# GAT layer and normalised-adjacency layer on one core: x and adjacency also given transposed, row sums as products with ones, scores on VectorE

## The chip, the cores and the metric

The kernel runs on one core of a Trainium2 chip. The metric is the device time of one execution in microseconds, lower is better. Times come from runs on the chip, as a median. The host builds the input arrays before the launch, and its work is not in the time.

## The reference

Two layers on 2048 nodes with 512 features. `adj` is a 2048 x 2048 matrix of zeros and ones, with many more edges at low node numbers.

```python
def _L0_gnn_ref(x, adj, W_seq, a1, a2, W_out, b_out):      # N 2048, H 16, DH 32
    seq = (x @ W_seq).reshape(N, H, DH)
    score1 = jnp.einsum('nhd,d->hn', seq, a1)
    score2 = jnp.einsum('nhd,d->hn', seq, a2)
    scores = score1[:, :, None] + score2[:, None, :]
    scores = jax.nn.leaky_relu(scores, negative_slope=0.2)
    scores = scores + (1.0 - adj)[None, :, :] * -65500.0
    attn = jax.nn.softmax(scores, axis=-1)
    hidden = jnp.einsum('hij,jhd->ihd', attn, seq).reshape(N, D_IN)
    return jax.nn.elu(hidden @ W_out + b_out)
...
def adjacent_mat(adj):                                      # adj here: (A + A.T) * 0.5
    adj = adj + jnp.eye(adj.shape[0], dtype=adj.dtype)
    deg = jnp.sum(adj, axis=1)
    dinv = jnp.where(deg > 0, deg ** (-0.5), 0.0)
    return dinv[:, None] * adj * dinv[None, :]
...
x = _layernorm(x + L0(x, adj, ...))
x = _layernorm(x + adj @ (adjacent_mat((adj + adj.T) * 0.5) @ x))
```

A row of `adj` without edges gets a softmax over all nodes, since every score in it is lowered by the same amount.

## The kernel before

Nodes go in 16 tiles of 128 (NT = 16), features in 4 chunks of 128 (KC = 4). All engines run programs of their own, tied together by semaphores. There are four stages.

**Preparation.** For each tile t of 128 rows, SyncE loads 128 rows of `x` (0.25 MB) and 128 rows of `adj` (1 MB), each into two buffers in turn. TensorE transposes the x tile (`x_transpose`, line 469, 4 instructions), multiplies it by W_seq (`seq_product`, line 477, 4 products of 512 columns in float32, each of which the profile shows as two matmuls), multiplies it by WA (line 484, for the two scores; WA is W_seq contracted with a1 and a2, built by VectorE in lines 838 and 840), and transposes the mask tile 128 x 128 by 128 x 128 (`mask_tiles`, line 496, 16 instructions). ScalarE casts the adjacency tile to bfloat16 and takes its row sums (`cast_adj`, line 664), moves seq out of PSUM (line 668) and half of the transposed mask (line 672). VectorE moves the transposed x (line 848), marks edgeless rows from the row sums and fills them with ones in the mask (lines 853 to 858), adds the tile to a running column sum (line 862), moves the scores (line 864), takes the largest |seq| per head (line 869) and moves the other half of the transposed mask into `MT` as 8-bit codes (line 873). `MT[:, j, :]` holds the mask with the neighbour index j*128.. on partitions; a one is the byte 56, which is 1.0 in fp8.

**Between preparation and attention.** TensorE transposes the scores S1 (line 523), ScalarE moves them (line 687), SyncE stores them and loads them back broadcast to all partitions (`load_s1`). VectorE reduces the maxima (lines 890, 892), GpSimd takes the maximum over partitions with `partition_all_reduce` (line 414), VectorE and ScalarE build the tables of exponentials (lines 899 to 917, ending with `tabs_done`), GpSimd multiplies seq by the tables (`prep(0)`, line 421), ScalarE rounds the result (line 700), VectorE forms the low parts (`low_operands(0)`, lines 923 and 925, ending with `pn_ready`), then the degrees (lines 993 to 997, `deg_done`), and enters `att_head(0)`.

**Attention.** 16 heads of 16 steps. In a step j, a sign row is made by ScalarE (line 711, 10 of 16 steps, in 4 buffers) or by VectorE (`own_step`, line 959, issued one step ahead, 6 of 16 steps), VectorE ands it with `MT` (lines 970 and 974, `g_ready`) into one of 16 slots, and TensorE does 48 matmuls of 66 columns from that slot (lines 553 to 556, `g_used`). Within a head VectorE also evacuates the sums of the head before (lines 930 to 950) and builds operands for the next one (lines 923, 925), GpSimd prepares the one after that (line 421).

**Output and second layer.** Output projection, layer norm, and two products of 16 x 16 x 2 matmuls of 512 columns (line 628). `restore_and_add` takes the filled rows out of the mask again with the row `NEB`, which had gone through DRAM.

## Time and profile before

| | |
|---|---|
| median of 3 runs | 840.22 us (839.98 to 841.34) |
| the profiled execution | 840.77 us, of which the span is 839.0 us |
| TensorE matmul busy | 778.6 us (93%), 14113 instructions |
| VectorE busy | 641.7 us (76%) |
| ScalarE busy | 460.5 us (55%) |
| GpSimd busy | 104.4 us (12%) |
| HBM read, written | 61.37 MB, 8.65 MB |

How to read it: the span is the time from the first to the last instruction on the core, and the execution's own time is 1.8 us longer. Matmuls are pipelined, so a busy TensorE is not one at its peak; the distance from one matmul's start to the next says more than the duration of one. The profile cuts the span into 40 slices of 21 us and gives the busy share of each in tenths. In the chain of waits each piece is what the next one waited for.

### The profile page before, as it was taken

The page shows a single profiled execution, that of the slowest core. Times are in us where ns is not written, and L with a number is a line of the kernel's source. Part 1 is how long each engine was busy: PE and PEld are TensorE (multiplying, and loading weights), DVE is VectorE, ACT ScalarE, POOL GpSimd, SP SyncE. Part 2 cuts the span into 40 slices and gives each one's busy share as a digit, 9 for nine tenths or more (in the row PEclk, how much of TensorE's full clock was granted, in tenths as well). Part 3 has the DMA queues.
Part 4 walks back from the last instruction along what each step waited for, and adds up shares of the span by engine and source line. Part 5 has one row for each costly group of instructions (what it writes and reads, how often), then busy time and mean ns, then how long its engine had stood idle before and what let it go on. Part 6 is the DMA issues. An engine that isn't in the chain of part 4 may idle for free.

```text
span 839.0 us, 31365 instructions
## 1 busy us (share of the span) xinstructions
PE 778.6 (93%) x14113; PEld 581.9 (69%) x14113; DVE 641.7 (76%) x927; ACT 460.5 (55%) x376; POOL 104.4 (12%) x98
## 2 busy tenths in 40 slices
PE   1999956999999999999999998998799999999996
PEld 0666636999999999999999998443234444444442
DVE  5677859999999999999999973799956666344444
ACT  2565639988898888888988880466421111100000
POOL 1000013111111110111111200144300000000000
PEclk9999987999999999999999999899879999999999
DMA  6456535111111011111101111421515553011110
GB/s 239 175 210 242 187 104 224 54 54 54 55 54 34 24 55 54 54 55 54 53 18 43 54 66 41 115 63 50 137 51 150 150 150 100 6 43 40 39 38 38
DMA packets 46502, 71.85 MB, mean 86 GB/s; under 512 B 1952, under 2 KB 34720, under 8 KB 42144
## 3 DMA queue, kind: packets, MB, share of 16 engines
q1 hardware_dynamic: 46384, 70.03, 25.1%
q8 instruction: 104, 1.70, 0.9%
q14 instruction: 14, 0.11, 0.0%
HBM read 61.37 MB, written 8.65 MB: 83 GB/s over the span
## 4 chain that ended last, share of the span: by engine, by line
PE 55%; issue 36%; POOL 4%; DVE 3%; DMA 1%; ACT 0%; POOLq 0%; SPq 0%; DVEq 0%; ACTq 0%
PE bank L556 15%; PE bank L555 15%; PE bank L553 14%; PE bank L477 7%; POOL RZ L444 2%; PE bank L496 2%; PE bank L484 2%; POOL rstd L440 2%; PE bank L469 1%; DMA AV<-in_L_gnn_a_dram 1%; DVE RZ L959 1%; DVE W L838 1%; DVE WA L840 1%; DMA RZ<-in_x_dram 0%; POOL RP L421 0%
## 5 line engine op out<-in xcount | busy, mean ns | idle before, releaser
L553 PE MATMUL bank<-RP,RG 128*128 128x66 f16 x4096 | 387.1, 193 | 16.8 <-DVE RG L970 16.8
L553 PEld LDWEIGHTS bank<-RP,RG 128*128 128x128 fp8e4 x4096 | 386.1, 98 | 19.4 <-issue 19.4
L556 PE MATMUL bank<-RP,MT 128*128 128x66 f16 x4096 | 387.1, 194 | 2.3 <-issue 2.3
L555 PE MATMUL bank<-RP,RG 128*128 128x66 f16 x4096 | 387.1, 195 | 0.0
L556 PEld LDWEIGHTS bank<-RP,MT 128*128 128x128 fp8e4 x4096 | 386.1, 98 | 0.0
L555 PEld LDWEIGHTS bank<-RP,RG 128*128 128x128 fp8e4 x4096 | 386.0, 97 | 0.0
L711 ACT ACTIVATE RZ<-RZ,TAB 128x2048 int8<-128x2048 f32 x160 | 306.0, 1988 | 5.8 <-DVE RG L970 4.8
L959 DVE TENSOR_SCALAR RZ<-RZ,TAB 128x2048 int8<-128x2048 f32 x96 | 133.0, 1385 | 0.0
L628 PE MATMUL bank<-RG,RP 128*128 128x512 f16 x512 | 116.4, 388 | 8.8 <-DVE RG L1102 7.5
L970 DVE TENSOR_TENSOR RG<-RZ,MT 128x512 int32<-128x512 int32 x160 | 121.1, 757 | 0.0
L628 PE MATMUL bank<-RZ,MT 128*128 128x512 f16 x512 | 110.7, 379 | 0.0
L628 PEld LDWEIGHTS bank<-RG,RP 128*128 128x128 bf16 x512 | 49.8, 99 | 75.7 <-DVE RG L1102 11.2
L628 PEld LDWEIGHTS bank<-RZ,MT 128*128 128x128 fp8e4 x512 | 50.0, 98 | 60.5
L421 POOL TENSOR_TENSOR RP<-SEQ,TAB 128x528 f32<-128x528 f32 x32 | 53.0, 1676 | 286.5 <-DVE RP L925 279.5
L477 PE MATMUL bank<-RZ 128*128 128x512 f32 x128 | 61.4, 624 | 8.3 <-DVE RZ L848 8.3
L974 DVE TENSOR_TENSOR RG<-RZ,MT 128x512 int32<-128x512 int32 x96 | 65.2, 680 | 0.0
L820 ACT ACTIVATE W<-bank 128x512 f32<-128x512 f32 x16 | 9.6, 597 | 99.2 <-PE bank L628 99.2
L599 PE MATMUL bank<-RZ 128*128 128x512 f32 x128 | 59.7, 611 | 0.0
L440 POOL TENSOR_TENSOR rstd<-vps,mhalf 128x1 f32<-128x1 f32 x32 | 21.1, 660 | 285.3 <-DVE vps L1093 217.5
L801 ACT ACTIVATE W<-bank,DSL 128x512 f32<-128x512 f32 x16 | 11.0, 687 | 75.0 <-PE bank L628 75.0
L1183 DVE SCALAR_TENSOR_TENSOR W<-bank,W 128x512 f32<-128x512 f32 x16 | 11.1, 691 | 51.7 <-ACT W L820 51.7
L700 ACT ACTIVATE RP<-RP 128x1056 f16<-128x1056 f32 x16 | 18.0, 1126 | 55.8 <-PE bank L556 49.3
(112 smaller groups left out, 672.0 us busy)
## 6 DMA issues: line engine op xcount, KB each, us to landing
RG<-in_adj_dram SPq DMA_DIRECT2D x16, 1024.0 KB, 4.9
RZ<-s_rows_dram SPq DMA_DIRECT2D x16, 1024.0 KB, 4.9
RP<-in_adj_dram SPq DMA_DIRECT2D x16, 1024.0 KB, 5.9
RZ<-in_x_dram SPq DMA_DIRECT2D x32, 256.0 KB, 2.6
seq_copy_dram<-SEQ SPq DMA_DIRECT2D x1, 4224.0 KB, 18.3
out_dram<-W SPq DMA_DIRECT2D x16, 256.0 KB, 2.0
RZ<-in_L_gnn_W_seq_dram SPq DMA_DIRECT2D x1, 1024.0 KB, 5.3
RZ<-in_L_gnn_W_out_dram SPq DMA_DIRECT2D x1, 1024.0 KB, 5.5
```

What stands on the lines that cost most here:

```text
L421: gp.tensor_tensor(V2[:, :, e, :], SEQ[:, :, h, :], tab[:, h, :].unsqueeze(2).broadcast_to([P, NT, DV]), ALU.mult).then_inc(v2_ready, 1)
L440: gp.tensor_tensor(rstd[:, u:u + 1], vps[:, u:u + 1], mhalf[:, 0:1], ALU.pow).then_inc(done, 1)
L477: last = mm(pb[2 + u][:, :], xT[:, u, k * P:(k + 1) * P], WS[:, k, :], start=(k == 0), stop=(k == KC - 1))
L553: mm(pb[bank][:, c:c + 2 * DV], step, high, start=(j == 0 and i % IB == 0), stop=(j == NT - 1), skip_group_check=True)
L555: mm(pb[bank][:, c:c + 2 * DV], step, low, start=False, stop=(j == NT - 1), skip_group_check=True)
L556: last = mm(pb[bank][:, c + DV:c + 3 * DV], mask, edge, start=False, stop=(j == NT - 1), skip_group_check=True)
L599: last = mm(pb[2 + u][:, :], hT[:, u, k * P:(k + 1) * P], WO[:, k, :], start=(k == 0), stop=(k == KC - 1))
L628: last = mm(pb[4 + 2 * u + l][:, :], stationary(j), moving[:, l, j, :], start=(j == 0), stop=(j == NT - 1))
L711: A(Z[:, m % NZ, :], S1B[:, u, :], ACT.Sign, bias=S2[:, h, j:j + 1], scale=-1.0).then_inc(z_ready, 1)
L959: V.tensor_scalar(ZD[:, (h * len(OWN) + m) % 2, :], S1B[:, u, :], S2[:, h, OWN[m]:OWN[m] + 1], -1.0, ALU.is_gt, ALU.mult).then_inc(zd_read ...
L970: V.tensor_tensor(G32[:, s, :], Z32[:, m % NZ, :], MT32[:, j, :], ALU.bitwise_and).then_inc(g_ready, 1)
L974: V.tensor_tensor(G32[:, s, :], ZD32[:, m % 2, :], MT32[:, j, :], ALU.bitwise_and).then_inc(g_ready, 1)
```

## The change

The host passes `x` and `adj` a second time, transposed (`x_t`, `adj_t`). The kernel reads `x_t` in 4 groups of 4 tiles (1 MB each) into four buffers, W_seq in 4 chunks, and 16 tiles of `adj_t` (1 MB each) into four buffers. ScalarE casts each tile of `adj_t` straight into `MT` as fp8, which also gives the column sums `CS`. Row sums come from 64 products of ones with `MT` (512 columns each), accumulated in 4 PSUM banks. The scores are products and a reduction on VectorE from seq. The maxima over partitions go through a TensorE transpose, a VectorE reduction, and a product with the identity that broadcasts them. Edgeless rows are found from the row sums (`find_empty`, `EMP`) and ored into `MT` in `fill_empty`, one step ahead within head 0; `restore_and_add` xors them away. The degrees move behind head 0, the scale factors ahead of head 15, and the flag for the rare general path is computed on VectorE alone. The x transposes, the mask transposes, the WA product, both `partition_all_reduce` and the trip of `NEB` through DRAM are gone.

```diff
@@ sync @@
-            for u in range(2):
-                load_x(u, u)
-                load_adj(u, u)
-            with sp.Fori(1, NT // 2) as p:
...
+            def load_adj(t):
+                if t >= NA:
+                    sp.wait_ge(adjb_done, t - NA + 1)
+                sp.dma_start(adj_f[:, t % NA, :], adj_t[t * P:(t + 1) * P, :]).then_inc(adj_in[t % NA], 16)
+            load_x(0)
+            for k in range(KC):
+                sp.dma_start(WS[:, k, :], w_seq[k * P:(k + 1) * P, :]).then_inc(wseq_in[k], 16)
...
+            load_adj(0)
+            load_x(1)
+            for t in range(1, NA):
+                load_adj(t)
+            load_x(2)
+            for t in range(NA, 2 * NA):
+                load_adj(t)
+            load_x(3)
+            for t in range(2 * NA, NT):
+                load_adj(t)
@@ gpsimd @@
-            gp.partition_all_reduce(VC[:, :], red[:, :, :].rearrange("p e h -> p (e h)"), P, RMAX).then_inc(allred, 1)
...
@@ tensor @@
+            for n in range(NT):
+                seq_product(n)
+                if n >= 2:
+                    score_row(n - 2)
+            row_sums(0, 4)
+            score_row(NT - 2)
+            score_row(NT - 1)
+            row_sums(4, 6)
+            pe.wait_ge(red_done, 1)
+            pe.wait_ge(seq_sb, NT)
+            tr(pb[0][0:3 * H, 0:P], red[:, :], idf[:, :]).then_inc(red_ps, 1)
+            row_sums(6, 8)
+            pe.wait_ge(top_sb, 1)
+            mm(pb[1][:, 0:3 * H], TOPB[:, :], idf[0:3 * H, 0:3 * H], start=True, stop=True).then_inc(top_ps, 1)
+            row_sums(8, 12)
...
+            for t in range(NT):
+                last = tr(pb[7][:, t:t + 1], ROWR[0:1, t * P:(t + 1) * P], idf[0:1, 0:1])
@@ scalar @@
+            def cast_adj(t):
+                sc.wait_ge(adj_in[t % NA], (t // NA) * 16 + 16)
+                A(MT8[:, t, :], adj_f[:, t % NA, :], ACT.Copy, saturate=False, accum_out=CS[:, t:t + 1]).then_inc(adjb_done, 1)
...
+            for n in range(NT):
+                move_seq(n)
+                if n % GT == 2 and n > GT:
+                    move_s1(n // GT - 1)
+                cast_adj(n)
+            move_s1(NT // GT - 1)
...
             high_operands(0)
+            for k in range(KC):
+                sc.wait_ge(emp_sb, k + 1)
+                A(ROWR[0:1, k * 512:(k + 1) * 512], pb[4 + k][0:1, :], ACT.Copy).then_inc(rowr_sb, 1)
@@ vector @@
+            def scores(t):
+                seq_t = SEQ[:, t, :, 0:DH]
+                ve.wait_ge(seq_sb, t + 1)
+                V.tensor_reduce(VMT[:, t, :], seq_t, AX.X, ALU.max, apply_absolute_value=True).then_inc(vm_done, 1)
+                if t >= 1:
+                    ve.wait_ge(s_sb, t)
+                V.tensor_tensor(PRD, seq_t.unsqueeze(1).broadcast_to([P, 2, H, DH]),
+                                AV[:, :, :].unsqueeze(2).broadcast_to([P, 2, H, DH]), ALU.mult).then_inc(products_done, 1)
+                ve.wait_ge(products_done, t + 1)
+                V.tensor_reduce(TAB[:, 0:2, :, t], PRD, AX.X, ALU.add).then_inc(s_sb, 1)
...
+                    if h == 0:
+                        if j < NT - 1:
+                            fill_empty(j + 1)
+                        ve.wait_ge(mt_full, j + 1)
                     ve.wait_ge(g_used, h * NT + (j + 1))
...
+            def find_empty(k):
+                ve.wait_ge(row_ps, k + 1)
+                V.tensor_scalar(EMP[:, k * 512:(k + 1) * 512], pb[4 + k][:, :], 0.0, ONE8, ALU.is_equal, ALU.mult).then_inc(emp_sb, 1)
+            def fill_empty(j):
+                V.tensor_tensor(MT32[:, j, :], MT32[:, j, :], EMP32, ALU.bitwise_or).then_inc(mt_full, 1)
             low_operands(0)
+            for k in range(KC):
+                find_empty(k)
+            ve.wait_ge(emp_sb, KC)
+            fill_empty(0)
+            att_head(0)
```

## Rows read from the trace of the kernel before

**Rows 1.** The profile's page: TensorE's busy tenths in 40 slices; DMA issues (KB, us to landing).

```profile
PE   1999956999999999999999998998799999999996
...
RG<-in_adj_dram SPq DMA_DIRECT2D x16, 1024.0 KB, 4.9
RP<-in_adj_dram SPq DMA_DIRECT2D x16, 1024.0 KB, 5.9
RZ<-in_L_gnn_W_seq_dram SPq DMA_DIRECT2D x1, 1024.0 KB, 5.3
```

**Rows 2.** Chain that ended last (start us, length us, what): one tile, last tile.

```profile
26.96 3.59 PE bank L477 x8
30.55 0.81 PE bank L484 x8
31.37 0.47 PE bank L469 x4
31.84 0.89 PE bank L496 x16
...
111.71 0.81 PE bank L484 x8
```

**Rows 3.** Groups by line and form, 0 to 125 us (busy us, mean ns).

```profile
L664 ACT ACTIVATE RZ<-RG 128x2048 bf16<-128x2048 f32 x16 | 30.4, 1903 | 10.9 <-DMA RG<-in_adj_dram 10.9
...
L848 DVE COPY RZ<-bank 128x512 f32<-128x512 f32 x16 | 11.1, 691 | 2.8 <-PE bank L469 2.8
...
L838 DVE TENSOR_TENSOR W<-RZ,AV 128x2048 f32<-128x2048 f32 x2 | 4.6, 2292 | 8.7 <-DMA AV<-in_L_gnn_a_dram 8.6
...
L869 DVE TENSOR_REDUCE RP<-SEQ 128x16 f32<-128x512 f32 x4 | 2.7, 674 | 0.0
```

**Rows 4.** Timeline 112 to 133 us: between preparation and attention.

```profile
115.09 0.41 DVE L892 TENSOR_REDUCE red<-TAB 128x16 f32<-128x256 f32 x1
...
117.32 0.29 DVE L905 TENSOR_SCALAR TAB<-TAB 128x256 f32<-128x256 f32 x1
...
119.75 0.07 DVE L917 MEMSET RD<- 128x16 f32 x1
...
123.07 2.12 POOL L421 TENSOR_TENSOR RP<-SEQ,TAB 128x528 f32<-128x528 f32 x2 [6.99 <-issue]
...
127.83 0.44 DVE L925 TENSOR_SCALAR RP<-RP 128x1056 f16<-128x1056 f16 x1
...
128.38 1.06 DVE L995 TENSOR_SCALAR ROW<-ROW 128x16 f32<-128x16 f32 x1
...
132.43 0.21 PE L553 MATMUL bank<-RP,RG 128*128 128x66 f16 x1 [16.78 <-DVE RG L970]
```

**Rows 5.** VectorE's timeline in attention: heads 0 to 2, head 15.

```profile
130.39 1.27 DVE L959 TENSOR_SCALAR RZ<-RZ,TAB 128x2048 int8<-128x2048 f32 x1
131.59 0.70 DVE L970 TENSOR_TENSOR RG<-RZ,MT 128x512 int32<-128x512 int32 x1
132.21 0.68 DVE L974 TENSOR_TENSOR RG<-RZ,MT 128x512 int32<-128x512 int32 x1
...
150.56 1.27 DVE L959 TENSOR_SCALAR RZ<-RZ,TAB 128x2048 int8<-128x2048 f32 x1
...
207.09 0.71 DVE L930 TENSOR_TENSOR RP<-bank,TAB 128x528 f32<-128x528 f32 x1 [0.83 <-PE bank L556]
...
498.05 0.71 DVE L930 TENSOR_TENSOR RP<-bank,TAB 128x528 f32<-128x528 f32 x1 [5.00 <-PE bank L556]
```

**Rows 6.** Window 136 to 137 us (us, busy by engine, PEclk, DMA share, GB/s).

```profile
136.00:137.00 1.00, 1.00 (x35) 1.00 (x33) 1.00 (x1) 1.00 (x1) 0.00 (x0) 0.96 1.11 473
```

**Rows 7.** Window 9 to 10 us (columns as in Rows 6).

```profile
9.00:10.00 1.00, 0.55 (x3) 0.58 (x4) 1.00 (x1) 0.00 (x0) 0.00 (x0) 1.00 1.04 442
```

**Rows 8.** Timeline (start us, us, engine line op): first tile's product.

```profile
18.83 5.96 PE L477 MATMUL bank<-RZ 128*128 128x512 f32 x8 [8.29 <-DVE RZ L848]
```

**Rows 9.** GpSimd, line 421, 110 to 200 us: what stood ahead of it.

```profile
L421 POOLq MODIFY_POOL_CONFIG  x2: 99/99/99, 116.0 to 116.1; - x2
```

More of the change, by code:

```diff
@@ L462, in _ @@
             mm, tr = nc.tensor.matmul, nc.tensor.transpose
[L463 to L474 removed]
+            pe.wait_ge(consts, 5)
@@ L529, in _, with score_row @@
-            pe.wait_ge(tiles_added, NT)
-            for j in range(NT):
-                last = mm(pb[7][:, j:j + 1], CSA[:, j * P:(j + 1) * P], ones[:, 0:1], start=True, stop=True)
-            last.then_inc(col_ps, 1)
+            def score_row(t):
+                g = t // GT
+                pe.wait_ge(s_sb, t + 1)
+                if g >= 2 and t % GT == 0:
+                    pe.wait_ge(s1T_sb, g - 1)
+                last = tr(pb[2 + g % 2][0:H, (t % GT) * P:(t % GT + 1) * P], S1[:, :, t], idf[:, :])
+                if t % GT == GT - 1:
+                    last.then_inc(s1T_ps, 1)
@@ new lines, in row_sum, with row_sums @@
+            def row_sum(t, k):
+                last = mm(pb[4 + k][:, :], ones[:, :], MT8[:, t, k * 512:(k + 1) * 512], start=(t == 0), stop=(t == NT - 1))
+                if t == NT - 1:
+                    last.then_inc(row_ps, 1)
+            def row_sums(lo, hi):
+                for t in range(lo, hi):
+                    pe.wait_ge(adjb_done, t + 1)
+                    for k in range(KC):
+                        row_sum(t, k)
+            for n in range(NT):
+                seq_product(n)
+                if n >= 2:
+                    score_row(n - 2)
@@ L909, in _ @@
+            own.mark(V.tensor_copy(SEQ[:, :, :, DH], VM.unsqueeze(1).broadcast_to([P, NT, H])))
+            own.mark(V.reciprocal(RV[:, :], VM))
             own.wait(ve)
@@ L1018, in _ @@
             ve.wait_ge(dscale, 3)
-            for h in range(2, H):
-                att_head(h)
+            att_head(H - 1)
             scale_sums(H - 1)
```

302 lines of the change are left out of this document (85 added, 217 removed).

## The prediction

> **What bounds the kernel now.** I read the page's 40 slices first: TensorE stands at 9 or above from slice 3 to 23, which is preparation and attention [rows 1]. Busy matmuls say little, so the chain that ended last comes next. It runs through preparation on TensorE alone, tile after tile: 3.59 us for the seq product, 0.81 for WA, 0.47 for the x transposes, 0.89 for the mask transposes, 5.76 us in all, and the last seq product ends at 111.71 us, where the last WA product starts [rows 2]. I call this moment T. The other engines have room: ScalarE's cast is 1.90 us of each tile, and of VectorE's operations the move of the transposed x is 0.69 and the largest |seq| 0.67 [rows 3].
>
> From T to the first attention matmul at 132.43 there are 20.7 us, a chain of small steps over all engines: maxima ready at 115.50 (115.09 + 0.41), tables' input at 117.61, `tabs_done` at 119.82, GpSimd's first product only at 123.07, `pn_ready` at 128.27, first matmul 132.43 [rows 4].
>
> In attention VectorE's timeline shows who leads. It waits for TensorE at line 930, the first evacuation of the head before: at 207.09 for head 2, at 498.05 for head 14. So a head takes TensorE (498.05 - 207.09) / 12 = 24.25 us. VectorE did its own head 0 from 130.39 to 150.56, 20.2 us, and is ahead of TensorE [rows 5]. Attention costs 24.25 us a head whatever VectorE does, as long as it keeps this lead. At the start TensorE ran at half its clock (1.2 of 2.4 GHz) from 132.43 until 136, for 3.6 us, so half of that, 1.8 us, was lost [rows 4, 6]. After attention nothing of the change lies on the path: a xor takes the place of an and of the same form.
>
> **Part 1, the preparation.** Removed from TensorE: WA, x and mask transposes, 2.17 us of 5.76 a tile. Added in the loop: one score transpose a tile; the four x transposes take 0.47 us, so one is 0.12 us [rows 2]. What is left is the seq product: between 3.4 us (an estimate: 3.59 less some 0.2 for the turn to another kind of product) and the 3.59 of the chain. I take 3.5, since nothing but one short transpose stands between two products.
>
> Who could be late instead? ScalarE: cast 1.90 + the seq move, under 0.7 = 2.6 us [rows 3]. VectorE: largest |seq| 0.67; the two score operations work on 1024 elements, and the one in line 838 takes 2.29 us for 2048, so at most 1.25 each with the start of an operation in it: 3.2 us a tile [rows 3]. This is under 3.6, but only by 0.4 us. Between the two ends (half of 2.29, all parallel: 2.9; a full 1.6 each for the odd strides: 3.9) I take 3.2. DMA: 1 MB of W, 4 of x, 16 of adjacency are 22.0 MB. With several loads queued 442 GB/s is moved, at a busy share of the DMA engines of 1.0 [rows 7]. Then 22.0 MB take 50 us, inside 58. The last buffers are asked for four tiles ahead, 14 us, while one load lands in 4.9 us when little else is queued [rows 1]. SyncE's queue holds the x loads behind adjacency loads that wait for casts; the latest, for tile 12, is behind load 7, which waits for cast 3, long before tile 12. So DMA is hidden.
>
> The Trainium skill speaks against this ("DMA: Bandwidth & Descriptors", "Where 436 GB/s comes from": the HBM side binds at some 358 GB/s for each core). By it the 22.0 MB would need 61 us, the last moves of seq would stand behind casts that wait for loads, and the sum would be about 1 us longer. The measured 442 GB/s decides.
>
> Start: W (1 MB) lands 5.3 us after its issue at about 0.7, at 6.0 [rows 1]. Now x group 0, of the same size and run length, is issued there, and the first quarter of W follows 0.6 us later (0.26 MB at 442 GB/s): 6.6. The clock is low at first: the first product took 5.96 against 3.59, so 2.4 us more [rows 2, 8]. T = 6.6 + 2.4 + 16 x 3.5 + 14 x 0.12 = 66.7 us (65.1 with 3.4; 68.2 with 3.59). Before it was 111.7: 45.0 us less.
>
> **Part 2, from T to attention.** The old steps and the new, each with the same kinds of rows:
> - To maxima ready: 3.8 us before. Now the seq move 0.65, the three score operations 3.1, and four small reductions and a negation instead of two reductions, 1.8: 5.5.
> - To the tables' input: 2.1 before, with GpSimd's all-reduce in it. Now two trips through PSUM: transpose 0.3, reduction 0.3, copy 0.2; then TensorE stands behind `row_sums(6, 8)`, 8 matmuls of 0.21 us (512 columns at 2.4 GHz) = 1.7, which is longer than VectorE needs; product 0.3, then five small operations 1.4: 3.8.
> - Tables: 2.2, unchanged [rows 4].
> - GpSimd's answer to `tabs_done`: before 3.25 us (119.82 to 123.07) although it stood idle [rows 4]. Ahead of the product stand two MODIFY_POOL_CONFIG at 116.0 [rows 9], just behind the all-reduce; 116.0 to 123.1 is a change of code. Without the all-reduce there is none: 0.1.
> - GpSimd, ScalarE, VectorE to `pn_ready`: 5.2 (123.07 to 128.27), unchanged [rows 4].
> - `pn_ready` to first matmul: 4.2 before [rows 4]. Now four `find_empty` of 512 elements from PSUM, each 0.6 (0.69 from line 848, about 0.08 less from start to start, like the ands at 131.59 and 132.21, 0.62 apart), then `fill_empty` 0.6, own_step 1.2, `fill_empty` 0.6, and 0.7, waits 0.2: 5.8 [rows 3, 5]. ScalarE's copies and first sign row (four copies in step with `find_empty`, then 0.6 and 2.0) end at 5.1, just in time.
>
> The sum is 22.6 us against 20.7. In the old path the little operation of line 995 took 1.06 us, about 0.9 too long, while GpSimd was at work on `prep(1)`, and another like it followed [rows 4]. If `find_empty` is held up in the same way it costs 1.7: 22.6 to 24.3. I take 23.0, near the low end, as `find_empty` reads PSUM and the one of line 995 reads SBUF. By the Trainium skill ("SBUF — State Buffer", "Who interferes with whom") an operation of VectorE with at most one SBUF input outside the two-port modes isn't held up by GpSimd, so that the sum would be 22.6; no row shows the case. The row sums are hidden: 64 x 0.21 = 13.7 us on TensorE from T, while `find_empty` asks for them at T + 16.8. The stored scores, two transfers that have 17 us, too.
>
> First attention matmul: 66.7 + 23.0 = 89.7, against 132.43: 42.7 us earlier.
>
> **Part 3, head 0.** VectorE gets 15 more `fill_empty` of 0.6 = 9.0 us. Its 20.2 us held about 1.7 of GpSimd's interference, which now falls behind head 0 with `deg_done`: 27.5 us. TensorE needs 24.25 + 1.8 for the low clock = 26.1. Step by step, VectorE first falls behind at step 12, after the low operands (1.6 us): slot 12 is ready 20.7 us after slot 0, and TensorE gets to it at 19.9; the slot for step 13 comes 2.4 us later against 1.5. Together 1.65 us are lost by the end of the head (0 if the fills run at 0.5; 4 if GpSimd's interference stays in head 0 and doubles). In head 1 VectorE works 22.7 us against 24.25 and is ahead again. `deg_done` now comes about 20 us later; behind it on GpSimd are the power (4.2) and `prep(2)`, for whose result ScalarE may wait 2 us in head 1; its four sign rows in store cover that. The scale factors, moved ahead of head 15, fall where VectorE waits 5.0 us for TensorE [rows 5].
>
> **Sum.** 42.7 - 1.65 = 41.0 us. The profiled execution took 840.77 (span 839.0, 1.8 around it), 0.55 above the median of the runs: 840.77 - 41.0 = 799.8, and against the median 799.2.
>
> **The rivals.**
> - VectorE bounds preparation (its tile 3.9 instead of 3.2): 16 x 0.3 = 5 us more, 804. For: only 0.4 us of room. Against: all pieces are continuous streams of shapes seen.
> - DMA paces preparation at 300 GB/s instead of 442: 73 us of load, 4.5 of start, last cast at 81, and ScalarE holds the seq moves behind the casts; T is then at about 78: 811. For: the 22 MB now come in 58 us, far denser than before. Against: rows 7.
> - GpSimd still answers 3.2 us late: 802.5.
> - TensorE starves in head 0 and its clock stays at the low level through it: 48 matmuls of 66 columns at 1.2 GHz are 2.64 us a step, 42.2 us a head, so 18 more: 817.
> - Slower than before: the loads don't overlap, and each MB takes what the strided adjacency loads take alone, 5.9 us [rows 1]. 21 x 5.9 + 4.5 = 128 us to the last load; the last seq move waits for the cast before the last, at 125; attention starts 22 us later, at 147, which is 14.6 us later than now, and head 0 adds 1.65: 857. It decides from 5.1 us for each MB, about 205 GB/s.
>
> **Chances.** Forecast 0.70, VectorE 0.10, DMA 0.08, GpSimd 0.05, clock 0.04, slower 0.03. The forecast's bounds: T 65.1 to 68.2, part 2 22.6 to 24.3, head 0 0 to 4: 795.5 to 804. With the rivals next to it the range is 794 to 811. Faster 0.96, within 0.2% 0.01, slower 0.03; 0.2% is about what a measurement here can tell from no change.
>
> **What would show it.** Distances of 3.5 to 3.6 us between seq products and the last one ended at 67; VectorE's tile of 3.2 us; GpSimd's product within 0.2 us of `tabs_done`; 23 us from T to the first matmul, 26 to 30 us for head 0 and 24.25 for each one after. If seq products wait for the seq move, or the moves for casts behind loads, part 1 is wrong; if VectorE waits never return in heads 1 to 3, part 3 is.

## The result, and the profile after

The changed kernel takes 798.5 us, the median of 4 runs (797.52 to 800.07), against 840.1 for the kernel before, measured beside it (839.85 to 841.34). The ratio is 0.9504, 95% interval 0.9485 to 0.9522. The prediction said 799.2, range 794 to 811. The profiled execution has a span of 797.1 us, 41.9 less than the 839.0 of before. I split these 41.9 at the first and the last product of attention.

First the page of the changed kernel: busy tenths of TensorE and the DMA engines in 40 slices of 20 us, then the loads of the adjacency (KB each, median us from issue to landing).

```profile
PE   6999799999999999999999997989699999999996
...
DMA  7992510111111011111011214122345551011111
...
RG<-in_adj_t_dram SPq DMA_DIRECT2D x16, 1024.0 KB, 10.6
```

Against rows 1, TensorE's gap has moved from slice 6 to slice 5, and a load of the adjacency takes 10.6 us to land instead of 4.9 or 5.9. The loads now lie close together, and the DMA digits of slices 2 and 3 are 9.

The chain that ended last (start us, length us, what), from the first product to the last scores.

```profile
7.03 12.96 PE bank L451 x24
20.09 3.44 PE bank L451 x8
23.53 0.11 PE bank L460
23.64 3.44 PE bank L451 x8
...
62.63 3.45 PE bank L451 x8
...
68.59 1.23 DVE TAB L796
```

This answers rows 2: where a tile was 5.76 us of four kinds of work, it is now one seq product and one score transpose (line 460), 3.545 us in the mean of 12 tiles ((62.63 - 20.09) / 12), and TensorE alone is on the chain for all 16 tiles. T, the end of the last seq product, is 62.63 + 3.45 = 66.1 us, against 111.7.

These 45.6 us have two parts. TensorE's first product starts at 7.03 instead of 18.83 us (rows 8), and from there to T it is 59.05 instead of 92.88. So 33.8 us come from the tiles and 11.8 from the start. In the kernel before, the chain of the start was the load of the attention vectors, then four operations of 2.3 us on VectorE that build WA, then the move of the first transposed x, which stood behind them in VectorE's program (the load and the first of the four):

```profile
1.78 6.74 DMA AV<-in_L_gnn_a_dram
...
8.62 2.30 DVE W L838
```

With WA gone, TensorE waits for x and the first quarter of W alone.

The timeline of the stretch behind it (start us, us, engine, line, operation; in brackets the idle time before it, and what ended it) answers rows 4.

```profile
70.98 0.42 DVE L809 TENSOR_REDUCE red<-TAB 128x16 f32<-128x256 f32 x1
...
74.10 0.21 DVE L817 COPY VC<-bank 128x48 f32<-128x48 f32 x1 [1.54 <-PE bank L488]
...
75.22 0.29 DVE L824 TENSOR_SCALAR TAB<-TAB 128x256 f32<-128x256 f32 x1
...
77.65 0.07 DVE L836 MEMSET RD<- 128x16 f32 x1
77.80 2.13 POOL L404 TENSOR_TENSOR RP<-SEQ,TAB 128x528 f32<-128x528 f32 x2 [75.51 <-DVE RD L836]
...
82.83 2.48 DVE L914 TENSOR_SCALAR EMP<-bank 128x512 int8<-128x512 f32 x4
82.99 2.10 POOL L404 TENSOR_TENSOR RP<-SEQ,TAB 128x528 f32<-128x528 f32 x2 [3.06 <-DVE RP L844]
...
88.79 0.22 PE L515 MATMUL bank<-RP,RG 128*128 128x66 f16 x1 [0.95 <-DVE RG L893]
```

The first attention matmul is at 88.79 instead of 132.43: 43.6 us earlier, 45.6 at T less 2.0 between T and attention (22.7 instead of 20.7). From there to VectorE's last evacuation it is 392.5 us (481.31 - 88.79) instead of 389.7 (522.12 - 132.43): 2.8 given back. What follows is 1.1 us shorter. 43.6 - 2.8 + 1.1 = 41.9.

Where the 2.8 are is read from the start of every 768th attention matmul, which begins a head (us for a head):

| head | 0 | 1 | 2 | 3 | 4 | 5 to 13 | 14 | 15 |
|---|---|---|---|---|---|---|---|---|
| before | 26.27 | 24.10 | 24.08 | 24.07 | 24.08 | 24.07 to 24.08 | 26.12 | 24.09 |
| changed | 27.68 | 25.01 | 24.34 | 24.07 | 24.80 | 24.07 to 24.08 | 25.67 | 24.09 |

Head 0 has 1.4 more and head 1 has 0.9 more. The differences of heads 4 and 14 (0.7 more, 0.5 less) are in stops in which TensorE waits for no semaphore; experiment 7 is about them. The 0.3 of head 2 is in no single wait. In heads 0 and 1 two things are seen. TensorE's granted clock is at its lower level, 1.2 GHz, for 5.0 us (to 93.8) instead of 3.6 (windows: us, busy us by engine, granted clock, DMA share, GB/s):

```profile
93.00:94.00 1.00, 1.00 (x25) 1.00 (x23) 1.00 (x3) 1.00 (x2) 0.00 (x0) 0.59 0.00 0
94.00:95.00 1.00, 1.00 (x38) 1.00 (x35) 1.00 (x3) 1.00 (x1) 0.00 (x0) 1.00 0.00 0
```

And TensorE waits for VectorE three times behind its first matmul, 1.3 us in all (the wait of 0.95 at 88.79 is ahead of it and so already counted):

```profile
109.57 0.20 PE L515 MATMUL bank<-RP,RG 128*128 128x66 f16 x1 [0.36 <-DVE RG L897]
...
111.97 0.20 PE L515 MATMUL bank<-RP,RG 128*128 128x66 f16 x1 [0.71 <-DVE RG L893]
...
136.96 0.20 PE L515 MATMUL bank<-RP,RG 128*128 128x66 f16 x1 [0.18 <-DVE RG L893]
```

The last of them is in head 1. Which of the two, clock or VectorE, sets the length of these heads is told by experiment 7: VectorE.

### The profile page after: what moved, and what is told of

Its sections match the earlier page's. It is cut to its first block, busy times and chain, and to the rows that moved or that the text cites. A ratio compares the mean times of both kernels' runs of the same rounds, so it can differ in the third digit from the quotient of the medians.

```text
span 797.1 us, 30149 instructions
## 1 busy us (share of the span) xinstructions
PE 756.9 (95%) x13731; PEld 552.4 (69%) x13731; DVE 617.8 (78%) x864; ACT 446.8 (56%) x364; POOL 96.4 (12%) x94
## 3 DMA queue, kind: packets, MB, share of 16 engines
q1 hardware_dynamic: 46064, 69.77, 25.4%
## 4 chain that ended last, share of the span: by engine, by line
PE 48%; issue 38%; DVE 7%; POOL 4%; DMA 1%; ACT 0%; POOLq 0%; SPq 0%; DVEq 0%; ACTq 0%
PE bank L518 14%; PE bank L517 13%; PE bank L515 13%; PE bank L451 7%; DVE RZ L878 2%; POOL RZ L423 2%; POOL rstd L419 2%; DVE RG L893 1%; DVE MT L918 1%; DVE RG L897 1%; DMA RZ<-in_L_gnn_W_seq_dram 1%; DMA RZ<-in_x_dram 0%; DVE RP L842 0%; PE bank L465 0%; DVE EMP L914 0%
## 5 line engine op out<-in xcount | busy, mean ns | idle before, releaser
L561 PE MATMUL bank<-RZ 128*128 128x512 f32 x128 | 59.2, 607 | 0.2 <-ACT RZ L678 0.2
L451 PE MATMUL bank<-RZ 128*128 128x512 f32 x96 | 44.9, 621 | 7.0 <-DMA RZ<-in_L_gnn_W_seq_dram 7.0
L561 PEld LDWEIGHTS bank<-RZ 128*128 128x128 f32 x128 | 23.7, 196 | 25.1 <-issue 23.8
## 6 DMA issues: line engine op xcount, KB each, us to landing
RG<-in_adj_t_dram SPq DMA_DIRECT2D x16, 1024.0 KB, 10.6
RZ<-in_x_t_dram SPq DMA_DIRECT2D x3, 1024.0 KB, 11.8
```

Of the source, the lines that this page charges most:

```text
L451: last = mm(pb[t % 2][:, :], XT[t // GT][:, k, (t % GT) * P:(t % GT + 1) * P], WS[:, k, :], start=(k == 0), stop=(k == KC - 1))
L561: last = mm(pb[2 + u][:, :], hT[:, u, k * P:(k + 1) * P], WO[:, k, :], start=(k == 0), stop=(k == KC - 1))
```

## The experiments

The kernel before, measured anew beside each set, took 839.1 to 841.4 us, so that times of different sets can be compared to some 0.3%, 2.3 us; where less matters, the traces decide. They scatter too. Six other profiles have the changed kernel's preparation untouched, and T is 64.9 to 66.4 us in them; from the last attention matmul to the end, the changed kernel and its eleven variants, all with the same code there, take 314.9 to 317.0 us.

**1. TensorE's old work put back.** The changed kernel, with WA's products and the x and mask transposes back in every tile, their results unread.

```
                for k in range(KC):
                    mm(pb[4][:, 0:2 * H], XT[t // GT][:, k, ...], idf[:, 0:2 * H], ...)
                for k in range(KC):
                    tr(pb[5][:, k * P:(k + 1) * P], XT[t // GT][:, k, ...], idf[:, :])
                for half in range(2):
                    ...
                        tr(bk[:, jj * P:(jj + 1) * P], idb[:, :], idb[:, :])
```

> The changed kernel with the work that left TensorE put back into its loop, its results unread: for each tile 8 matmuls of 32 columns in float32 (the old WA product), 4 transposes of the x tile, 16 bfloat16 transposes of 128 columns. Theory (TensorE's own work sets the preparation): each tile grows from 3.55 by 0.81 + 0.47 + 0.89 = 2.17 us, T moves from 66.0 by 16 x 2.17 = 34.7 us, nothing after T changes: 798.5 + 34.7 = 833.2, so that 7 of the 41.6 us come from elsewhere (start and GpSimd). Rival (the gain came from VectorE's and ScalarE's part, which also shrank): much less than 34.7 comes back, under 20 us, below 818.

Measured: 832.8 us (832.37 to 832.96), ratio 0.9897, interval 0.9878 to 0.9916. The chain has the tile of before again:

```profile
36.85 0.89 PE bank L461 x16
...
42.57 0.89 PE bank L461 x16
```

42.57 - 36.85 = 5.72 us, and the first attention matmul is at 123.08, 34.3 us later than in the changed kernel. So 34.3 of the 41.6 us come from TensorE's shorter tile alone, whatever else was rearranged.

**2. x transposed alone.** The kernel before with only the x half of the change: TensorE keeps WA and the mask transposes, and the four x transposes go, with VectorE's move behind them.

```
-                sp.dma_start(xs[:, u, :], x[DS(t * P, P), :]).then_inc(x_in[u], 16)
+                sp.dma_start(xT[:, t % 4, :].rearrange("p (k i) -> p k i", k=KC),
+                             x_t[:, t * P:(t + 1) * P].rearrange("(k p) i -> p k i", p=P)).then_inc(x_in[t % 4], 16)
...
-                    tr(pb[u][:, k * P:(k + 1) * P], xs[:, u, k * P:(k + 1) * P], idf[:, :])
```

> The kernel before with one part of the change: x comes transposed from the host, into four buffers; the x transposes on TensorE and VectorE's move of them are gone, all else stays. Theory: 16 x 0.47 = 7.5 us less in TensorE's tiles, and at the start the first product no longer waits for the move that stood behind the building of WA on VectorE (18.0 us); now only the WA product does, so that another 6.5 us go: 840.2 - 14 = 826. Rival (only the transposes' own time goes, as the first tile waits for WA all the same): 832.5. Rival (nothing goes, as mask transposes then wait for VectorE): 838 or more.

Measured: 829.3 us (825.27 to 829.39), ratio 0.9841, interval 0.981 to 0.9871: between the two expectations. The chain:

```profile
18.45 1.79 PE bank L476 x8
...
21.95 5.29 PE bank L469 x8
27.24 0.81 PE bank L476 x8
...
28.94 3.49 PE bank L469 x8
```

The tile is 5.19 us (3.49 + 0.81 + 0.89) as the theory has it, and T is 99.95 against 111.71. But TensorE is done with its first product long before WA is built, and behind that wait its granted clock is 0.50, from 18.6 to 25.4 us: 1.79 us instead of 0.81 for WA's product, 5.29 instead of 3.49 for the seq product, and with the mask transposes between them 3.6 us are lost, which the theory hadn't in its sum. In the full change this wait is gone, as WA is.

**3. Which engine is next: half of the products, and the score product twice.** One run leaves two of the four feature chunks of each seq product out, so that TensorE needs half. The other leaves nothing out, and VectorE does each tile's product with the attention vectors twice.

```
-                for k in range(KC):
+                for k in range(2):
```

```
-                V.tensor_tensor(PRD, seq_t..., ALU.mult).then_inc(products_done, 1)
+                for i in range(2):
+                    V.tensor_tensor(PRD, seq_t..., ALU.mult).then_inc(products_done, 1)
```

> The changed kernel with half of the seq product left out (2 of 4 chunks of features are summed, so seq is another matrix). TensorE's tile falls from 3.55 to about 1.85 us. Theory: the next bounds lie just below TensorE, VectorE's three score operations at 3.16 us a tile and the loads (1.25 MB a tile at 412 GB/s, 3.2 us), so that the maxima are ready at about 11 + 16 x 3.16 + 1.8 = 63.4 instead of 71.4: 8 us less, 790.5 (788 to 793). Rival (TensorE far above all else): 16 x 1.7 = 27 us less, 771. Rival (DMA already at its limit in the changed kernel, which its busy share of 1.0 from 10 to 50 us could mean): under 3 us less, above 795.

> The changed kernel with the score product on VectorE issued twice a tile: VectorE's tile goes from 3.16 to 4.4 us, above TensorE's 3.55. Theory (VectorE has 0.4 us of room a tile and no more): scores end at 13.9 + 16 x 4.4 = 84.3 instead of 69.8, 14.5 us more, 813. Rival (VectorE's part is hidden with room to spare, since TensorE waits only for scores two tiles back): under 7 us more, below 806.

Each of the two has a single run. Half the products: 795.2 us, so 3.3 less and not 8. The chain of this run says who took over:

```profile
15.66 13.28 DMA RG<-in_adj_t_dram
...
59.74 1.14 DVE RP L793
...
62.72 1.14 DVE RP L793
...
65.45 2.96 PE bank L465 x8
```

Until 41.6 us it is the loads (ScalarE waits 10.5 us for them, 4.2 in the changed kernel), then VectorE with a tile of 2.98 us (62.72 - 59.74). The scores end at 65.1 instead of 69.8, and of these 4.7 us 1.2 are lost again where the first row sums take 2.96 instead of 1.73: TensorE had been idle for a third of the time (busy 6.35 of the 10 us from 40 to 50), and its granted clock is 0.50 from 65.8 to 69.2. Three resources lie within a few us of each other here: TensorE, DMA, VectorE.

The product twice: 812.5 us, expected 813. The sum came out by other terms than expected, though: TensorE waits 9.5 us for VectorE in this stretch, since a VectorE tile is now 4.24 us; the scores end at 81.4, 11.6 later and not 14.5, and the row sums start at a granted clock of 0.50 again (3.41 and 2.30 instead of 1.73 each), which brings 2.3 more. So VectorE's room in the changed kernel is 3.545 - 2.98 = 0.57 us a tile, and it is used up by one more operation of 1.2.

**4. The code change on GpSimd.** The prediction booked 3.2 us for leaving out the all-reduce. One run puts it back in place of the two trips through PSUM. Another keeps the trips and adds an unread all-reduce behind the input of the tables.

```
+            gp.wait_ge(red_done, 1)
+            gp.partition_all_reduce(VC[:, :], red[:, :], P, bass.bass_isa.ReduceOp.max).then_inc(top_ps, 1)
```

```
+            gp.wait_ge(texp_in, 1)
+            gp.partition_all_reduce(RSC[:, :], red[:, :], P, bass.bass_isa.ReduceOp.max)
```

> The changed kernel with the maxima over partitions taken by GpSimd's all-reduce again, in place of the two trips through TensorE and PSUM; all else as changed. Theory (a change of code on GpSimd stands between the all-reduce and its first product, 7.0 us from the one's end to the other's start): tables are ready 2.4 us earlier than the 77.7 of the changed kernel, but GpSimd starts its product at 71.5 + 0.5 + 7.0 = 79.0 instead of 77.8: 1.2 us more, 799.7. Rival (the 3.2 us before were GpSimd's slow wake-up after a long wait, whatever it did): it stays below 798.5 by up to 2.4 us: 796.

> The changed kernel with one all-reduce on GpSimd whose result nobody reads, issued when the tables' input is ready (75.5). Theory: GpSimd's first product can't start before 75.5 + 0.5 + 7.0 = 83.0 instead of 77.8, 5.2 us more: 803.7. Rival (the all-reduce costs its own half microsecond and is over before tabs_done): no change, 798.5.

With the all-reduce back: 801.0 us (800.19 to 803.04), ratio 0.9543. With the unread one: 807.6 us (806.51 to 808.23), ratio 0.9616. GpSimd's timeline of the first, then of the second:

```profile
70.74 0.50 POOL L408 PARTITION_ALL_REDUCE VC<-red  x1 [68.19 <-DVE red L805]
78.37 2.12 POOL L404 TENSOR_TENSOR RP<-SEQ,TAB 128x528 f32<-128x528 f32 x2 [7.13 <-issue]
```

```profile
75.93 0.50 POOL L409 PARTITION_ALL_REDUCE RSC<-red  x1 [73.38 <-DVE TAB L827]
86.29 2.12 POOL L405 TENSOR_TENSOR RP<-SEQ,TAB 128x528 f32<-128x528 f32 x2 [9.85 <-issue]
```

An all-reduce is followed by 7.13 us in which GpSimd does nothing, and in the changed kernel, without one, its product starts 0.08 us after `tabs_done` (77.72). From the maxima (`red`) to GpSimd's product are 7.8 us with it (78.37 - 70.60) and 6.4 without (77.80 - 71.40): the net gain of this part is 1.4 us, and not 3.2, since the trips cost more than the all-reduce itself. From T to the first attention matmul it is the same 1.4 (24.1 against 22.7). The medians differ by 2.5, 1.3 more than expected; that rest is within the scatter of T and of the time behind attention. The prediction had both terms (3.2 for the pause, 1.7 against it for the trips), so its sum was right. The second run missed its expectation by 3.9 us: the pause was 9.85 us there. In that run the DMA engines are at a share of 1.04 from 76 to 86 us, with the copy of seq in flight from 78, against 0.72 in the pause of the first run:

```profile
76.00:86.00 10.00, 5.36 (x25) 2.25 (x23) 1.26 (x6) 0.97 (x3) 0.44 (x1) 0.93 1.04 439
```

The runs show that the pause comes with the all-reduce. That it is a load of code that queues with other traffic fits both numbers, but no run here isolates it: in neither pause, nor in that of the kernel before, does the DMA view list a packet of an instruction queue.

**5. Head 0 without the fills.** The 16 operations that mark edgeless rows in the mask are left out.

```
-                    if h == 0:
-                        if j < NT - 1:
-                            fill_empty(j + 1)
-                        ve.wait_ge(mt_full, j + 1)
...
-            fill_empty(0)
```

> The changed kernel without the 16 fills of edgeless rows (the or's are left out, rows are still found). Theory: the first and of head 0 stays where it is, within 0.2 us, because ScalarE's first sign row arrives at 87.8 in any case; in head 0 VectorE no longer falls behind, so that TensorE's waits of 2.2 us in head 0 go: 796.3 (795.5 to 797). Rival (the 2.9 us that attention costs more than before come from the longer low clock, 5.0 us instead of 3.6, and from its own stalls): under 1 us less, 797.8 or more. Rival (the fills sit on the path twice): 3.5 us less, 795.

Measured: 797.1 us (796.49 to 797.46), ratio 0.9493, interval 0.9472 to 0.9513. This is just above the range of the theory. Behind the first attention matmul TensorE's waits for VectorE fall from 1.3 us to nothing; head 0 takes 26.76 us instead of 27.68, head 1 24.68 instead of 25.01. What remains is the wait for the first slot, where ScalarE's sign row is now late:

```profile
87.59 0.69 DVE L889 TENSOR_TENSOR RG<-RZ,MT 128x512 int32<-128x512 int32 x1 [1.30 <-ACT RZ L662]
```

So the fills cost 1.25 us in the two heads, although they are 9 us of work. The medians differ by 1.4, which alone could not be told from their spread.

**6. The order at the start of attention.** `find_empty` ahead of `low_operands(0)`.

```
+            for k in range(KC):
+                find_empty(k)
             low_operands(0)
-            for k in range(KC):
-                find_empty(k)
```

> The changed kernel with find_empty put ahead of low_operands(0), into a stretch in which VectorE waits. By the count of operations the first and starts 2.1 us earlier (797.9 minus something: 796.4). Theory (GpSimd's prep(1), 2.1 us from pn_ready on, holds up VectorE's operations that use two SBUF inputs or read SBUF at double rate, and does not hold up find_empty, which reads PSUM): prep(1) now meets the fills and own_step, each of its two operations costs VectorE 0.85 us, and of the 2.1 us 0.4 are left: 798.1. Rival (no such difference): 796.4.

Measured: 797.3 us (797.12 to 797.81), ratio 0.9495, between theory and rival, so that the timeline has to decide. `tabs_done` to the first slot of VectorE is 9.80 us instead of 10.30. The timeline shows what is won and what is lost again:

```profile
82.37 3.47 POOL L404 TENSOR_TENSOR RP<-SEQ,TAB 128x528 f32<-128x528 f32 x2 [3.58 <-DVE RP L844]
82.80 2.10 DVE L878 TENSOR_SCALAR RZ<-RZ,TAB 128x2048 int8<-128x2048 f32 x1
84.82 1.56 DVE L918 TENSOR_TENSOR MT<-MT,EMP 128x512 int32<-128x512 int32 x1
```

The four `find_empty` (2.5 us) lie in VectorE's idle time now. But where they stood, beside GpSimd's `prep(1)`, there are operations that read SBUF, and these are held up: 2.10 us instead of 1.28, 1.56 instead of 0.69, and GpSimd's pair takes 3.47 instead of 2.10. In the changed kernel `find_empty`, which reads PSUM, runs 0.69 us beside the same GpSimd pair, and so does neither harm. Both sides' delays are seen in one place here, and VectorE's two eat 1.7 of the 2.5 us.

**7. Two cheap ideas that should have gained 3 to 6 us, and what they found.** One run starts TensorE earlier (the load of x's first tile is split off) and has one more tile of row sums behind the product for the maxima. One fills TensorE's idle time ahead of attention with 86 unread matmuls, to keep its clock up. One does both, with 24 matmuls ahead of tile 0 as well.

```
-            load_x(0)
+            sp.dma_start(XT[0][:, :, 0:P], xk[:, :, 0:P]).then_inc(x_first, 16)
...
+            sp.dma_start(XT[0][:, :, P:GT * P], xk[:, :, P:GT * P]).then_inc(x_in[0], 16)
...
-            row_sums(6, 8)
+            row_sums(6, 7)
```

```
+            for i in range(72):
+                mm(pb[0][:, 0:P], ones[:, :], idb[:, :], start=True, stop=True)
             for t in range(NT):
                 last = tr(pb[7][:, t:t + 1], ...)
...
+            for i in range(14):
+                mm(pb[0][:, 0:P], ones[:, :], idb[:, :], start=True, stop=True)
```

> The changed kernel with two orders changed: the load of x's first group is split, so that the 128 columns of tile 0 (0.25 MB) arrive first, then W_seq, then the rest; and one more tile's row sums (row_sums(7)) come behind the product for the top half instead of ahead of it. Nothing is left out. In the changed kernel's profile TensorE starts at 7.03 us, and the row that answers to the top maxima waits for TensorE, which is 1.1 us behind by then. Theory (TensorE is on the path of all 16 tiles and of the two maxima): TensorE starts some 2.8 us earlier, if W_seq's first quarter lands with the tile, and the top product ends 0.9 us earlier, of which the table builder's end keeps about 0.9: time 797.5 - 2.8 - 0.9 = 794 to 795 us. Rival (the 16 MB behind it hold the casts and the tiles, as the run with half the products showed DMA at 0.98 to 1.03 of its span): what the start gives is waited away for the adjacency before tile 15, and less than 1.5 us remains: 796 to 797.5 us.

> The changed kernel plus 86 matmuls of 128 columns, unread, on TensorE in the stretch between the row sums and the first attention matmul, where it stood idle: 72 ahead of the transposes of the row factors and 14 behind them. Nothing is left out. In the changed kernel's profile the first 5.0 us of attention run at 1.2 GHz (granted clock 0.50), so about 2.5 us are lost there. Theory (the idle gap is what the clock falls for, and TensorE's clock is on the path): the granted clock is near 1.0 in the first microseconds of attention, TensorE gets up to 2.5 us back, of which VectorE's pace in head 0 (it ends its part at 114 us, 2.2 us of waits) takes some 0.5 to 1: 795.5 to 797 us. Rival (VectorE alone sets head 0, so TensorE only waits longer for it): waits for VectorE grow by as much as the clock gives, and the time stays at 798 to 799 us, though the clock is up.

> Both of the other two runs of this set together, and 24 matmuls of 128 columns on the constants, unread, ahead of tile 0 while the first loads are on the way, so that the tiles too start at full clock. Nothing is left out. If the gains add (start 2.8, top product 0.9, start clock 1.8, attention's clock 1.5 to 2) the time would be 798.5 - 7 = 791 to 792 us; the loads set a floor for the end of the tiles, since with half of the products left out the scores ended only 4.7 us earlier. Theory: 792 to 794 us. Rival (the loads take back what the start gives): 795 to 797 us, with TensorE waiting for VectorE's copies or for fp8 casts before the last tiles.

Measured: 798.6 us (797.28 to 798.91) for the early start, 804.1 (802.03 to 804.96) for the filled gap, 807.0 (806.39 to 809.93) for both. All three are above what theory and rival expected.

The early start: TensorE begins at 4.30 us instead of 7.03, but T is 65.5 instead of 66.1. The chain gives the reason: it begins with an adjacency load, and TensorE waits 1.1 us for a seq move behind the cast of that load.

```profile
6.10 14.06 DMA RG<-in_adj_t_dram
...
22.81 3.67 PE bank L454 x8
```

The split loads push the adjacency back. Of the 2.7 us at the start nothing is left at T that can be told: six profiles with the old order of loads have T at 64.9 to 66.4. From T to attention it is 21.8 us instead of 22.7, the 0.9 that was expected of the moved row sums, and the median shows nothing that can be told from its spread.

The filled gap: the clock is at 2.4 GHz from the first attention matmul on, at 87.72. And yet head 0 takes 27.69 us and head 1 25.00, as in the changed kernel (27.68 and 25.01), and VectorE's first evacuation comes 35.5 us after the first matmul in both. In the changed kernel and every variant of it that has the fills, heads 0 and 1 end 52.7 us after the first attention matmul, at whichever clock they start: VectorE sets them, so the clock is worth nothing there. That explains no gain, but not the loss of 5.6 us. The loss is spread over the heads. From 160 to 440 us TensorE's waits are, with the filled gap:

```profile
PE bank L522 <- issue: 3.9, 5, 1.5
PE bank L521 <- issue: 1.7, 3, 0.7
...
```

In the changed kernel the same stretch has a single one of 0.5. TensorE stops once in nearly every head, for no semaphore, and heads 5 to 13 take 24.83 us in the mean instead of 24.08. The DMA view of the stretch around such a stop names what it waits for. The changed kernel from 302.4 to 307.2 us, around the 1 MB load of one head (queue, packets, MB, share):

```profile
q1 hardware_dynamic: 143, 1.05, 57.3%
q8 instruction: 2, 0.03, 3.6%
```

With the filled gap, from 302.6 to 308.4, it has no row for the instruction queue:

```profile
q1 hardware_dynamic: 143, 1.05, 52.4%
```

To half a microsecond, the packets of the instruction queue come every 4.0 us in the changed kernel, at 302.5, 306.5, 310.5; with the gap filled they come at 302.0, 308.5, 311.5, with 6.5 us across the load, which is on the engines from 304.5 to 308. TensorE stopped at 310.1 for 0.65 us. The page has 104 such packets with 1.70 MB, so 16 KB each, and TensorE has 27,462 matmuls and weight loads: about 64 bytes for each. 128 matmuls with their weight loads fill a packet, a head is 768 matmuls, six packets exactly, and so the fetches fall at the same place in every head. What that place is, the number of instructions ahead of attention decides.

The last run tests this: the filled gap again, with 128 unread matmuls instead of 86.

```
-            for i in range(72):
-                mm(pb[0][:, 0:P], ones[:, :], idb[:, :], start=True, stop=True)
+            for i in range(54):
+                mm(pb[0][:, 0:16], ones[:, :], idb[:, 0:16], start=True, stop=True)
+            for i in range(60):
+                mm(pb[0][:, 0:P], ones[:, :], idb[:, :], start=True, stop=True)
```

> The run with the filled gap again, with 128 unread matmuls in place of 86: 54 of 16 columns and 60 of 128 ahead of the transposes of the row factors, 14 behind them. Nothing is left out. The run with 86 had TensorE at full clock from the first attention matmul and took 804.1 us, 5.6 more than the changed kernel: TensorE stopped once in nearly every head for 1.0 to 1.8 us with no instruction to wait for, and in the traces the instruction queue (packets of 16 KB, one per 4 us of attention) shows a gap of 6 to 7 us over each head's 1 MB row load, where the changed kernel's fetches fall just ahead of the load and behind it. The packets times their size over the matmuls and weight loads give 64 bytes for each, so that 128 matmuls with their weight loads are one packet, and 86 shift the fetches by two thirds of one. Theory (the stops are fetches caught behind the row load, and where they fall is set by the count of instructions ahead): with 128 the fetches fall as in the changed kernel, the stops go, and the time is 797 to 799.5 us; the clock of head 0 gives nothing, as VectorE sets its pace. Rival (the filled gap itself, by its work or by the higher clock, makes the stops): they stay, and the time is 803 to 805.5 us.

Measured: 797.9 us (796.63 to 799.62), ratio 0.95, interval 0.9485 to 0.9514. More matmuls of the same kind (though 54 are of 16 columns, so that the columns are 10,336 against 11,008), and 6.2 us less. TensorE's waits from 160 to 440 us, and the DMA view from 302.8 to 308:

```profile
PE bank L524 <- issue: 0.8, 1, 0.8
```

```profile
q8 instruction: 2, 0.03, 4.1%
```

The fetches are back at 4 us (303.0, 307.5, 311.0) and the stops are gone. Also with 128 the clock is up from the first attention matmul (1.00 in the windows from 88 us), heads 0 and 1 end 52.7 us after it, and the time is that of the changed kernel.

Four runs of this record change the count of matmuls ahead of attention by something else than whole packets, and they can be set beside each other:

| run | matmuls more | beyond whole packets of 128 | stops under "issue", 160 to 440 us | heads 5 to 13, mean |
|---|---|---|---|---|
| changed kernel | 0 | 0 | 1, 0.5 us | 24.08 |
| 128 unread | 128 | 0 | 1, 0.8 us | 24.08 |
| old work put back (experiment 1) | 448 | 64 | 2, 1.7 us | 24.26 |
| half of the products (experiment 3) | -64 | 64 | 3, 2.1 us | 24.32 |
| filled gap | 86 | 86 | 9, 6.6 us | 24.83 |
| both ideas | 110 | 110 | 9, 9.5 us | 25.32 |

The last row is also the reason of the 807.0 us of that run. So it was the phase of TensorE's instruction fetches against the head's 1 MB load, and neither the work nor the clock. What isn't settled is why the fetch is late: whether its packet waits behind the load's packets on one DMA engine or in the memory.

## Why the prediction was right, point by point

**T.** Predicted 66.7, measured 66.1. TensorE's first product starts at 7.03 instead of 6.6, as the chain has W's first quarter landing at 6.89 (issued at 1.25, 5.64 to land). The slow start costs 12.96 - 3 x 3.44 = 2.6 (predicted 2.4): up to 12 us a matmul comes every 0.86 us and then every 0.43, while the granted clock reads 1.00 throughout, so that here the rows show the slow pace and not its clock. A product is 3.44 instead of 3.5 and a score transpose 0.11 instead of 0.12, and that makes 1.2 us in the other direction. All this is no more than the scatter of T between profiles. VectorE's tile was predicted at 3.2 and is 2.98 when nothing holds it (experiment 3), so the rival of a VectorE-bound preparation had 0.57 us of room against it instead of 0.4.

**DMA.** Predicted as hidden, and it is, but less comfortably than "50 us inside 58" says. From 10 to 50 us the DMA share is 0.98 to 1.03 at 398 to 420 GB/s, less than the 442 of rows 7, and the loads end at about 58 us. ScalarE waits 4.2 us for them. One window:

```profile
40.00:50.00 10.00, 10.00 (x26) 4.22 (x25) 8.48 (x10) 6.94 (x11) 0.00 (x0) 1.00 1.01 420
```

The step that took a single microsecond of 442 GB/s as a rate for 50 us was too hopeful by 5 to 10%. It cost nothing here, since TensorE needed the time. The 358 GB/s of the Trainium skill ("DMA: Bandwidth & Descriptors", "Where 436 GB/s comes from") do not hold in this kernel, where one core moved more than that through four windows of 10 us. The experiments that lightened TensorE or started it earlier ran into the loads at once.

**From T to attention.** Predicted 23.0, range 22.6 to 24.3; measured 22.7 (88.79 - 66.08). By the steps of the prediction: maxima ready 5.3 (5.5), tables' input 4.1 (3.8; TensorE was behind by the 1.54 us of line 817, as foreseen, and a little more), tables 2.2 (2.2), GpSimd's answer 0.1 (0.1), `pn_ready` 5.1 (5.2), first matmul 5.9 (5.8; its terms as written add up to 5.7). The open point was whether GpSimd's `prep(1)` holds `find_empty` up. It doesn't: four in 2.48 us beside it, where an operation that reads SBUF takes 0.8 us more (experiment 6). So the low end was the better value, and taking 23.0 between the two cases added 0.4 that isn't there. The nearest row was of an operation of the other kind. The low end is also what follows from the Trainium skill ("SBUF — State Buffer", "Who interferes with whom"), and the trace agrees with it.

**Heads 0 and 1.** Head 0 was worked out well: 26.1 + 1.65 = 27.7 us predicted, 27.68 measured. Slot 12 was to be ready 20.7 us after the first and slot 13 2.4 us later; TensorE waits at 20.8 (109.57 - 88.79) and 2.40 later. The low clock was taken over from rows 6 as 3.6 us and was 5.0, which changed nothing, since VectorE sets this head. Against the kernel before, whose head 0 took 26.27, the loss is 1.4.

The step that failed is the next one, that in head 1 "VectorE works 22.7 us against 24.25 and is ahead again". VectorE enters head 1 at 114.13, 2.3 us ahead of TensorE, and loses this lead beside GpSimd, whose `prep(2)` and `prep(3)` both fall into this head, since `prep(2)` now comes behind the power (one operation beside each):

```profile
118.36 1.56 DVE L893 TENSOR_TENSOR RG<-RZ,MT 128x512 int32<-128x512 int32 x1
...
133.29 2.12 DVE L878 TENSOR_SCALAR RZ<-RZ,TAB 128x2048 int8<-128x2048 f32 x1
```

These two and the ands behind each of them (1.56 and 1.58 instead of 0.69) take 0.8 to 0.9 us longer each than elsewhere. TensorE waits once more at 136.96, and head 1 takes 25.01 us instead of 24.10: 0.9 that the sum did not have. The prediction moved GpSimd's interference out of head 0 and priced only ScalarE's wait in head 1. It had also named a sign, that VectorE's waits for TensorE return in heads 1 to 3. VectorE's timeline:

```profile
238.95 0.71 DVE L849 TENSOR_TENSOR RP<-bank,TAB 128x528 f32<-128x528 f32 x1
263.03 0.71 DVE L849 TENSOR_TENSOR RP<-bank,TAB 128x528 f32<-128x528 f32 x1 [1.23 <-PE bank L518]
287.11 0.71 DVE L849 TENSOR_TENSOR RP<-bank,TAB 128x528 f32<-128x528 f32 x1 [1.24 <-PE bank L518]
```

At this line they return only at 263.03, with the evacuation of head 6. VectorE's pace of 22.75 us a head (147.75 to 170.52 to 193.26) was predicted well (22.7), but it gains only 1.33 a head on TensorE's 24.08, from a lead of nothing at 136.96. By its own sign this part of the prediction was wrong, and it was: not in the pace, but in where VectorE starts to gain.

**A head's time.** The 24.25 us that the prediction read from rows 5 are 24.08 in an undisturbed head (287.11 - 263.03). Between the two rows of before lies one stop of TensorE of 1.9 us under "issue": (498.05 - 207.09 - 1.9) / 12 = 24.09. It had next to no effect on the sum, since a stop at this place is on both sides (head 14: 26.12 before, 25.67 after), but the figure held something that is not the head's.

**The sum.** 43.6 (predicted 42.7) - 2.8 (1.65) + 1.1 behind attention (0) = 41.9 (41.0). The earlier start was underestimated by 0.9: 0.6 at T and 0.3 behind it. Of the 2.8, 1.4 are head 0, 0.9 head 1 and 0.5 the balance of TensorE's stops, of which the prediction had the first alone. The 1.1 behind attention is no gain of the change that could be told: with the same code there, profiles differ by 2.0 us (314.9 to 317.0). The granted clock goes with it, for it is 0.50 for 6.8 us behind attention in the kernel before and for 3.4 in the changed one, and of the changed kernel's profiles the single one with 6.8 (the all-reduce put back) is the longest. That the total came within 0.9 is in part luck, as an error of 1.15 in attention stands against 0.9 and 1.1 on the other side.

**The rivals.** None came. The run with the product doubled shows how the first would have looked, and the run with half the products how near the second was. The third, GpSimd still late, was rightly held unlikely: the pause comes with the all-reduce (experiment 4) and left with it. The fourth asked for a low clock all through head 0, and it ended after 5.0 us.

## What to carry to other kernels

When layout work goes off an engine that a stage waits for, sum the new tile for each other engine and for DMA, and write down the room of each: here they were 0.57 us a tile for VectorE and a few us in all for the loads, and this told what every later idea was worth. Before filling idle time to win back the clock, look at who sets the pace in the stretch behind it. Before reading a microsecond out of two profiles, see how much stretches with the same code differ between profiles. And if a change moves the time of a long, regular stretch that it doesn't touch, compare the "issue" waits and the instruction queue's packets before looking for a mechanism in the change.

## What the hardware showed that I had not expected

- TensorE's instructions come by DMA in packets of 16 KB, one for 128 matmuls with their weight loads, every 4.0 us in attention. When a fetch falls into a 1 MB load, TensorE can stop for 0.4 to 1.6 us; fetches only 5 to 6 us apart mostly cost nothing. As this repeats in each head, 86 more instruction pairs ahead of the loop cost 5.6 us of 798, and 128 cost nothing. An edit that changes the count of matmuls can gain or lose this much, and neither the kernel before nor the changed one had more than a few single stops.
- The longest single stops are of the same kind: 1.9 us at 490.6 in the kernel before, 1.4 at 451 in the changed one. The instruction queue's packets lie 7.5 us apart there (482.5 to 490.0, to half a microsecond) and 6.5 us (443.5 to 450.0), across the loads of W_out and b_out, 1.3 MB. The changed kernel from 443 to 452 us:

```profile
RZ<-in_L_gnn_W_out_dram SPq DMA_DIRECT2D x1, 1024.0 KB, 5.4
```

- The pause of GpSimd behind an all-reduce is 7.1 us at a DMA share of 0.72 and 9.85 us at 1.04.
- Interference of VectorE and GpSimd goes both ways: beside operations that read SBUF, GpSimd's pair takes 3.47 us instead of 2.10, and VectorE's operations take 0.8 to 0.9 us more each.
